# Transformer block with mixture of experts: weights as the stationary operand in gate and up, and f16 down products for the last 22 token tiles

## The reference, cut to what matters

```python
x = layernorm(x + attention(x))                  # 4 x 512 tokens, 256 wide, 16 heads
probs = softmax(x @ router_w.T); top_w, top_i = top_k(probs, 2); top_w /= top_w.sum()
for e in range(8):                               # 8 experts, 512 hidden columns
    gate = x @ ws[e, :512].T
    up   = x @ ws[e, 512:].T
    h    = silu(gate) * up
    out += combine[:, e:e+1] * (h @ w2s[e].T)    # 512 -> 256
x = layernorm(x + out)
```

## Time and profile before

| | us |
|---|---|
| median of 3 runs | 513.27 |
| lowest, highest | 512.68, 515.3 |
| the profiled execution, its own time | 515.15 |
| its span | 513.3 |
| mean granted TensorE clock | 0.947 |
| PE busy, PEld busy | 433.3, 264.0 |
| DVE, ACT, POOL busy | 334.8, 313.9, 244.5 |

### The profile page before, as it was taken

How to read it: one execution, slowest core, us unless ns; L and a number is a source line. 1 busy time by engine, 2 the same in 40 slices (tenths; PEclk the granted TensorE clock), 3 DMA queues, 4 the chain that set the end, 5 groups by cost and what they waited for, 6 DMA issues and landing times.

```text
span 513.3 us, 9836 instructions
## 1 busy us (share of the span) xinstructions
PE 433.3 (84%) x3058; PEld 264.0 (51%) x3058; DVE 334.8 (65%) x1184; ACT 313.9 (61%) x460; POOL 244.5 (48%) x332
## 2 busy tenths in 40 slices
PE   1999898999796999889973899999999999999700
PEld 0555444445453555445532567666666666666500
DVE  7156987876779887977698424577657666762234
ACT  0486549997866677665997167555535666653115
POOL 0063411123565487555825375644555665554322
PEclk9999969999999999979996799999999999999955
DMA  8368899822246214412321024333343333343254
GB/s 274 69 166 246 258 353 330 255 77 63 63 123 213 93 52 141 122 41 85 124 83 32 10 35 91 73 66 49 53 63 53 59 57 55 62 63 43 28 167 173
DMA packets 32978, 57.25 MB, mean 112 GB/s; under 512 B 5025, under 2 KB 23585, under 8 KB 31394
## 3 DMA queue, kind: packets, MB, share of 16 engines
q1 hardware_dynamic: 18306, 39.60, 24.6%
q0 software_dynamic: 7488, 10.27, 12.9%
q10 hardware_dynamic: 7136, 6.77, 4.2%
HBM read 38.64 MB, written 17.97 MB: 110 GB/s over the span
## 4 chain that ended last, share of the span: by engine, by line
PE 44%; DVE 23%; DMA 18%; issue 8%; ACT 6%; POOLq 1%; ACTq 0%; POOL 0%; SPq 0%; DVEq 0%
DMA sum_rows<-PT,IDXA 16%; PE PS L1587 9%; DVE PS L995 8%; PE PS L298 6%; PE PS L1614 5%; PE PS L1366 4%; PE PS L1405 4%; PE PS L1440 3%; PE PS L1387 2%; PE PS L305 2%; ACT PT L779 2%; DVE W L1132 2%; PE PS L1606 2%; PE PS L1459 1%; ACT W L817 1%
## 5 line engine op out<-in xcount | busy, mean ns | idle before, releaser
L995 DVE CUSTOM_DVE_ANT_0 PS<-PS,CB 128x512 f32<-128x512 f32 (+3 forms) x256 | 121.2, 516 | 35.2 <-PE PS L1366 33.9
L1587 PE MATMUL PS<-W,PT 128*128 x468 | 114.9, 382 | 4.0 <-issue 3.9
L779 ACT ACTIVATE PT<-PS 128x1024 f32<-128x1024 f32 x80 | 81.3, 1021 | 36.8 <-PE PS L1388 36.3
L730 POOL DMA_INDIRECT sum_rows<-PT,IDXA x39 | 62.1, 1593 | 57.6 <-DMA sum_rows<-PT,IDXA 21.4
L1366 PE MATMUL PS<-KQ 96*128 96x512 bf16 (+3 forms) x256 | 64.5, 316 | 13.1 <-DVE MX L995 11.9
L1587 PEld LDWEIGHTS PS<-W,PT 128*128 128x128 f16 x468 | 43.8, 98 | 43.2 <-issue 6.5
L1387 PE MATMUL PS<-KQ 104*128 104x512 bf16 (+3 forms) x256 | 60.8, 308 | 0.4 <-ACT PT L779 0.4
L714 POOL DMA_INDIRECT KQ<-x_rows,IDXA x39 | 40.0, 1027 | 30.4 <-DVE WS L1249 18.1
L1405 PE MATMUL PS<-PT,VA 128*32 128x256 f32 (+3 forms) x512 | 45.0, 446 | 4.7 <-ACT PT L779 4.7
L1388 PE MATMUL PS<-CB 128*128 128x128 bf16 x256 | 48.1, 223 | 0.0
L1366 PEld LDWEIGHTS PS<-KQ 96*128 96x128 bf16 x256 | 20.0, 100 | 46.3 <-DVE MX L995 33.4
(11 more groups left out here) (230 smaller groups left out, 891.4 us busy)
## 6 DMA issues: line engine op xcount, KB each, us to landing
W<-w1T SPq DMA_DIRECT2D x8, 1024.0 KB, 8.5
qk_parts<-W SPq DMA_DIRECT2D x32, 192.0 KB, 3.2
KQ<-qk_parts SPq DMA_DIRECT2D x32, 192.0 KB, 2.9
KQ<-qk_parts SPq DMA_DIRECT2D x64, 64.0 KB, 3.0
x_rows<-X1S ACTq DMA_DIRECT2D x4, 516.0 KB, 3.6
W<-xT SPq DMA_DIRECT2D x4, 512.0 KB, 6.7
KQ<-qk_parts SPq DMA_DIRECT2D x16, 128.0 KB, 3.0
sum_rows<-X ACTq DMA_DIRECT2D x4, 512.0 KB, 3.2
```

The source lines that it names most:

```text
L730: pool.indirect_dma_start(acc_dram, bass.IndirectOffsetOnAxis(ap=IDXA[:, j, 0:1], axis=0), YS[j % TRIO], None, compute_op=ALU.add).then_in ...
L779: act.activation(PT[n][:, :], STb[slot_of(k, n)].rearrange("p a n -> p (a n)"), ACT.Exp).then_inc(s["exp"], 1)
L995: last = dve.tensor_tensor_reduce(src, src, maskS[:, TT * P - w:], 1.0, LOW, ALU.add, ALU.max, MX[p][:, h, i:i + 1])
L1587: last = mm(dst, XGT[j % TRIO][:, x_part, k, :], w1h[:, bass.ds(at, UNIT)], start=(k == x_part == w_part == 0), stop=(k == KC - 1 and x_pa ...
```

## The change

- **Gate and up.** The operands change places: a block of 128 weight columns is stationary and the 128 token columns of `XGT` are streamed. 24 matmuls of 128 columns replace 6 of 512, twice per tile. The result has the hidden columns on the partitions, so the product DVE makes is already what down needs.
- **No transposes of the hidden part.** The 4 f32 or 8 f16 transposes of a tile and the copies out of them are gone, and so are the row maximum and its reciprocal.
- **Down.** Tiles 0 to 16 keep the f32 product. Tiles 17 to 38 (17 to 33 before) take the three f16 products; their input is scaled by a bound for each expert that `bounds` makes on DVE once, from the squares of the weights.
- **Order.** down(j-1) follows up(j) in every tile, and `add_result(j-1)` in every step of POOL. ACT's `down_squares` and `down_high` stand ahead of the last batch's other steps.

```diff
-SPLIT_FROM = 17
-LAST = NTILES - 5
-NSPLIT = LAST - SPLIT_FROM
-HSCALE = 2.0 ** -14
+SPLIT_FROM = NEARLY
+NSPLIT = NTILES - SPLIT_FROM
 N2 = FF // P * NX * E // 512
+HBOUND = 2.0 ** 8
...
-                if 1 <= j <= SPLIT_FROM or j > LAST + 1:
+                if j:
                     add_result(j - 1)
-                elif SPLIT_FROM + 2 <= j <= LAST:
-                    add_result(j - 2)
-                elif j == LAST + 1:
-                    add_result(j - 2)
-                    add_result(j - 1)
-                if j == 5 + 1:
+                if j == 6:
...
             def hidden_high(j):
-                i = j - SPLIT_FROM
-                act.wait_ge(f["ri"], i + 1)
-                act.activation(HHI[i % 2], HH, ACT.Copy, scale=RI[:, i:i + 1]).then_inc(f["hhi"], 1)
-
-            def hidden_columns(j):
-                act.wait_ge(f["th2"], j - SPLIT_FROM + 1)
-                act.wait_ge(f["yp"], j)
-                act.activation(HTH[:, 0, :, :].rearrange("p k t -> p (k t)"), HPh[0], ACT.Copy).then_inc(f["hta"], 1)
+
+                act.wait_ge(f["h"], j + 1)
+                if j >= SPLIT_FROM + 2:
+                    act.wait_ge(f["yp"], j - 1)
+                act.activation(HHI[j % 2], HH, ACT.Copy).then_inc(f["hhi"], 1)
...
+            for j in range(SPLIT_FROM, NTILES):
                 silu(j)
                 if j + 1 < NTILES:
                     columns(j + 1)
-                if j == LAST + 1:
-                    split_result(LAST - 1)
-                result(j - 1)
-            result(NTILES - 1)
+                if j == SPLIT_FROM:
+                    result(j - 1)
+                hidden_high(j)
+                if j > SPLIT_FROM:
+                    split_result(j - 1)
+            split_result(NTILES - 1)
...
+            def bounds():
+
+                dve.memset(STEP9[:, :, 0:1], 1.0)
+                dve.memset(STEP9[:, :, NX:NX + 1], 0.0)
+                link(dve.tensor_tensor(STEP9[:, :, 1:NX], CT[:, 0:NX - 1].unsqueeze(1).broadcast_to([P, NSPLIT, NX - 1]),
+                                       jidx[:, 0:NSPLIT].unsqueeze(2).broadcast_to([P, NSPLIT, NX - 1]), ALU.is_le))
+                link(dve.tensor_tensor(PICK8[:, :, :], STEP9[:, :, 0:NX], STEP9[:, :, 1:NX + 1], ALU.subtract))
+                link(dve.tensor_tensor(PICK8[:, :, :], PICK8[:, :, :], S8[:, :].unsqueeze(1).broadcast_to([P, NSPLIT, NX]), ALU.mult))
+                link(dve.tensor_reduce(SJ[:, :], PICK8[:, :, :], AX.X, ALU.add))
+                dve.wait_ge(s["sc2"], 2)
+                dve.tensor_scalar(WSJ[:, :], SJ[:, :], CC[:, :], None, ALU.mult)
+                link(dve.reciprocal(RSJ[:, :], SJ[:, :]))
+                link(dve.tensor_scalar(HSJ[:, :], RSJ[:, :], HBOUND, CW[:, :], ALU.mult, ALU.mult))
...
-                if i == 0:
-                    dve.wait_ge(f["th"], SPLIT_FROM)
-                else:
+                if i:
                     dve.wait_ge(f["hlo"], i)
-                dve.scalar_tensor_tensor(HH, U, CW[:, :], SIL, ALU.mult, ALU.mult).then_inc(f["h"], 1)
-                dve.wait_ge(f["h"], j + 1)
-                link(dve.tensor_reduce(HM[:, i:i + 1], HH, AX.X, ALU.max, apply_absolute_value=True))
-                link(dve.tensor_scalar(HB[:, i:i + 1], HM[:, i:i + 1], 1e-30, HSCALE, ALU.max, ALU.mult))
-                dve.reciprocal(RI[:, i:i + 1], HB[:, i:i + 1]).then_inc(f["ri"], 1)
-                dve.wait_ge(f["ws"], j + 1)
-                dve.scalar_tensor_tensor(WS2[:, i:i + 1], WS[:, j:j + 1], HB[:, i:i + 1], CC[:, :], ALU.mult, ALU.mult).then_inc(f["ws2"], 1)
+                dve.scalar_tensor_tensor(HH, U, HSJ[:, i:i + 1], SIL, ALU.mult, ALU.mult).then_inc(f["h"], 1)
 
             def hidden_low(j):
 
-                i = j - SPLIT_FROM
-                dve.wait_ge(f["hhi"], i + 1)
-                dve.scalar_tensor_tensor(HLO[i % 2], HH, RI[:, i:i + 1], HHI[i % 2], ALU.mult, ALU.subtract).then_inc(f["hlo"], 1)
-
-            def hidden_columns(j):
-
-                dve.wait_ge(f["th2"], j - SPLIT_FROM + 1)
-                dve.wait_ge(f["yp"], j)
-                dve.tensor_copy(HTH[:, 1, :, :].rearrange("p k t -> p (k t)"), HPh[1]).then_inc(f["htd"], 1)
+                dve.wait_ge(f["hhi"], j - SPLIT_FROM + 1)
+                if j >= SPLIT_FROM + 2:
+                    dve.wait_ge(f["yp"], j - 1)
+                dve.tensor_tensor(HLO[j % 2], HH, HHI[j % 2], ALU.subtract).then_inc(f["hlo"], 1)
...
+                dve.scalar_tensor_tensor(HT[j % 2], U, CW[:, :], SIL, ALU.mult, ALU.mult).then_inc(f["h"], 1)
                 if j == 0:
                     post(B - 1, 1, TB[1])
-                dve.wait_ge(f["th"], j + 1)
-                if j:
-                    dve.wait_ge(f["yp"], j)
-                dve.tensor_copy(HT.rearrange("p k t -> p (k t)"), HP).then_inc(f["ht"], 1)
...
             def half(j, e, dst, n, done):
 
-                for k in range(KC):
-                    for x_part, w_part in ((0, 0), (0, 1), (1, 0)):
-                        at = (e + k * NX) * (4 * UNIT) + (2 * n + w_part) * UNIT
-                        last = mm(dst, XGT[j % TRIO][:, x_part, k, :], w1h[:, bass.ds(at, UNIT)], start=(k == x_part == w_part == 0), stop=(k == KC - 1 and x_part == 1))
+                for c in range(FF // P):
+                    for k in range(KC):
+                        for w_part, x_parts in ((0, (0, 1)), (1, (0,))):
+                            at = (e + k * NX) * (4 * UNIT) + (2 * n + w_part) * UNIT + c * P
+                            for x_part in x_parts:
+                                last = mm(dst[:, c * P:(c + 1) * P], w1h[:, bass.ds(at, P)], XGT[j % TRIO][:, x_part, k, :],
+                                          start=(k == x_part == w_part == 0), stop=(k == KC - 1 and w_part == 1))
                 last.then_inc(done, 1)
...
-            def hidden_T(j):
+            def down(j, e):
                 pe.wait_ge(f["h"], j + 1)
-                if j:
-                    pe.wait_ge(f["ht"], j)
-                for k in range(FF // P):
-                    last = nc.tensor.transpose(HP[:, k * P:(k + 1) * P], HH[:, k * P:(k + 1) * P], ident)
-                last.then_inc(f["th"], 1)
-
-            def down(j, e):
-                pe.wait_ge(f["ht"], j + 1)
                 if j:
                     pe.wait_ge(f["ys"], j)
                 for k in range(FF // P):
-                    last = mm(YP[:, 0:E], HT[:, k, :], W2[k][:, bass.ds(e * E, E)], start=(k == 0), stop=(k == FF // P - 1))
+                    last = mm(YP[:, 0:E], HT[j % 2][:, k * P:(k + 1) * P], W2[k][:, bass.ds(e * E, E)], start=(k == 0), stop=(k == FF // P - 1))
                 last.then_inc(f["yp"], 1)
 
-            def split_hidden_T(j):
...
+            def split_down(j, e):
                 i = j - SPLIT_FROM
-                if i:
-                    pe.wait_ge(f["hta"], i)
-                    pe.wait_ge(f["htd"], i)
-                else:
-                    pe.wait_ge(f["ht"], SPLIT_FROM)
                 pe.wait_ge(f["hhi"], i + 1)
                 pe.wait_ge(f["hlo"], i + 1)
-                for r, part in enumerate((HHI[i % 2], HLO[i % 2])):
-                    for k in range(FF // P):
-                        last = nc.tensor.transpose(HPh[r][:, k * P:(k + 1) * P], part[:, k * P:(k + 1) * P], IDH[:, :])
-                last.then_inc(f["th2"], 1)
-
-            def split_down(j, e):
-                i = j - SPLIT_FROM
-                pe.wait_ge(f["hta"], i + 1)
-                pe.wait_ge(f["htd"], i + 1)
                 pe.wait_ge(f["ys"], j)
                 if i == 0:
                     pe.wait_ge(s["lo2"], N2)
                 for k in range(FF // P):
-                    for h_part, w_part in ((0, W2H), (0, W2L), (1, W2H)):
-                        last = mm(YP[:, 0:E], HTH[:, h_part, k, :], w_part[k][:, bass.ds(e * E, E)],
-                                  start=(k == 0 and h_part == 0 and w_part is W2H), stop=(k == FF // P - 1 and h_part == 1))
...
+                    for w_part, h_parts in ((W2H, (HHI, HLO)), (W2L, (HHI,))):
+                        for h_part in h_parts:
+                            last = mm(YP[:, 0:E], h_part[j % 2][:, k * P:(k + 1) * P], w_part[k][:, bass.ds(e * E, E)],
+                                      start=(k == 0 and w_part is W2H and h_part is HHI), stop=(k == FF // P - 1 and w_part is W2L))
...
+            for j in range(NTILES):
+                if j == NEARLY:
+                    pe.wait_ge(s["tab"], 2)
                 e = expert(j)
                 gate(j, e)
-                rows_T(j + 1)
+                if j + 1 < NTILES:
+                    rows_T(j + 1)
                 if j == 0:
                     out_proj(r, 0, (s["atc"], r * 2 + 1), TB[0])
                 up(j, e)
                 if j == 0:
                     out_proj(r, 1, (s["atc"], r * 2 + 2), TB[1])
-                if j:
+                if 1 <= j <= SPLIT_FROM:
                     down(j - 1, e_before)
```

(63 more changed lines are left out.)

74 lines of the change are left out of this document (12 added, 62 removed).

## The result

| | before | after |
|---|---|---|
| median of 4 runs, us | 513.14 | 551.26 |
| lowest, highest | 512.68, 515.3 | 550.31, 552.48 |
| ratio of the times, 95% interval | | 1.0735 (1.0697 to 1.0774) |
| profiled execution, its own time | 515.15 | 552.48 |
| its span | 513.3 | 550.7 |

Ratios leave out single runs more than 1.5% over the fastest of their own kernel (one of the four of e2_fused, three of the twelve of e8_fused_again); medians and ranges are of all runs. The kernel before was measured again beside the experiments and had 515.29 us beside e1 to e4 and 514.24 beside e5 to e8, so a difference between an experiment and the kernel after is sure to some 2 us only.

The account below looks back on a forecast made before the run. PE's sequencer was to bound the expert part: 289.7 + 91.8 (17 plain tiles) + 123.9 (21 split) + 1.5 + 2.5 = 509.4, last scatter-add at 510.2, 20.9 us later than before. Forecast 534 us, range 524 to 550.

Parts of the forecast that it names:

- What bounds: Expert part: PE's sequencer decides, with 32 register instructions a tile for gate and up in place of 8, 124 ns each.
- Start of tile 1: Value load of tile 1, no longer held by tile 0's hidden part: 289.7 us, bounds 288.5 and 291.8.
- The working of a tile: Sum of the sequencer's work in one tile: 5.90 us for a split tile, 5.40 for a plain one.
- Three distances make 0.36 to 0.38 us, 124 ns each: Price of a register instruction in gate and up, read from one trace window; 32 by 0.124 is 3.97 us a tile.
- Extras: PE's work beside the tiles (out projection, routing, counts, a few stalls): 2.5 us, bounds 0 and 6.
- The scatter chain is off the path: Scatter-adds into `sum_rows` no longer set the pace, since tiles of 5.4 and 5.9 us are over 4.59.
- its scatter-add starts 0.8 later: After the last down ends at 509.4, the last scatter-add starts 0.8 us later, at 510.2.
- The 81 ns a pair of the Trainium skill: Rule for sustained 128-column pairs, against the 56 ns used: plain tiles array-bound at 5.84 us, forecast 541.
- The array is the bound: Rival: 124 ns is waiting for a queue slot; plain tiles 4.64 us, split ones 4.59, about 501 us; 6%.
- pairs go slower: Rival: over long runs pairs exceed 56 ns, weight loads no longer hidden; 562 us at 98 ns, 538 at 77; 10%.
- The clock: Rival: the granted clock falls to 1.2 GHz as the array is busy; 8 us a tile, over 600 us; 2%.
- PE's instructions arrive too slowly: Rival: a split tile has some 175 instructions on PE against 96, and their arrival limits it; 550 us; 3%.

Follow-up runs that it names:

- e2_fused: Kernel after with gate and up addresses computed four at a time, 17 register instructions a tile in place of 32: 508.05 us, ratio to before 0.9859.
- e8_fused_again: The kernel of e2_fused measured once more in five rounds, 12 runs: 507.18 us, ratio to before 0.9838.
- e1_static: Kernel after with gate and up reading expert 0's weights at constant addresses in every tile, same matmuls: 507.72 us, ratio to before 0.9857.
- e4_more_pairs: Kernel after with sixteen more weight load and matmul pairs a tile at addresses already in registers, results unused: 555.52 us, ratio to before 1.0785.
- e5_plain: Kernel after with the plain f32 down product in all tiles but the last: 541.54 us, ratio to before 1.0535.
- e3_before_cut: Kernel before with its 512 streamed weight columns cut into four blocks of 128, each with its own address: 567.39 us, ratio to before 1.1015.
- e7_fused_noscatter: The kernel of e2_fused without the scatter-adds, a POOL memset in their place: 493.04 us, ratio to before 0.9591.
- e6_noscatter: Kernel after without the 39 scatter-adds, a one-column POOL memset in their place: 544.38 us, ratio to before 1.059.

## Why the prediction was right and where it failed

**What bounds.** Right. Register instructions stand 124 ns apart in the kernel after: the median of 1171 neighbours, with its quarters at 124 and 125, with one matmul or two behind them, and in e4_more_pairs, with two behind each, too. Taking 15 of 32 away (e2_fused) gives back 43 us, taking all away (e1_static) as much, and adding 24 to the kernel before (e3_before_cut) takes 52. That e1_static and e2_fused come out at the same time is in part chance: in both the scatter chain of the prediction, its 4.59 us a tile, stands behind the saving, but e2_fused without it (e7_fused_noscatter) keeps 4.60 us a tile, so there the sequencer needs as much as the chain.

**Start of tile 1.** 289.7 forecast, 289.9 measured. That it agrees to 0.2 is luck: in the experiments with the changed order this load starts between 287.7 (e5_plain) and 291.1 (e7_fused_noscatter).

**The working of a tile.** Right as a floor. If for each of the sequencer's steps in a tile the shortest distance to the next over 19 split tiles is taken, and these are added up, it is 5.90 us, the sum of the prediction; the same for the plain tiles of e5_plain is 5.42, against 5.40.

**The step that failed: "Three distances make 0.36 to 0.38 us, 124 ns each", carried over to all 32.** It was read in one place without a gap. Some distances are longer by 15 to 155 ns, most by 30 to 90. In the split tiles between 396 and 515 us there are 98 of them in 19 tiles, and the mean tile is 6.25 where the floor is 5.90: 0.35 us a tile. The trace of before had them too, under the array's work, where they cost nothing; I measured the distances in a gapless stretch and did not ask for the mean over many. By 37 tiles it is 12.7 us of the 16.7.

**Extras.** 2.5 forecast. The 17 periods of the plain part have 99.8 us: 17 by 5.42 is 92.1, gaps of 0.33 make 5.6, and 2.1 is left. Right.

**The second step that failed: "The scatter chain is off the path", "its scatter-add starts 0.8 later".** That holds up to tile 37. From the last value load to the last scatter-add the prediction has 5.90 + 1.5 + 0.8 = 8.2 us; it is 12.1. Kernel after, timeline of all engines at the end:

```profile
520.22 0.75 DVE L1268 SCALAR_TENSOR_TENSOR PT<-PS,HSJ,PT 128x512 f32<-128x512 f32 x1 [3.72 <-PE PS L1558]
...
521.00 0.63 ACT L916 ACTIVATE PT<-PT 128x512 f16<-128x512 f32 x1 [2.27 <-DVE PT L1268]
...
521.66 0.69 DVE L1275 TENSOR_TENSOR PT<-PT 128x512 f16<-128x512 f32 x1 [0.70 <-ACT PT L916]
...
522.56 0.39 PE L1591 MATMUL PS<-VR,PT 128*128 x2 [0.95 <-DVE PT L1275]
...
524.08 0.47 ACT L922 ACTIVATE PT<-PS,WS 128x256 f32<-128x256 f32 x1 [1.96 <-PE PS L1591]
```

In every other tile the chain product, high part, low part (the 2.5 us that I costed at nothing) is hidden by a whole gate and up; behind the last up there is only down(37), and PE stands 0.95 us for the low part. Then down(38) follows down(37) by 2.4 us and not by 6.2, so its result, ready at about 524.6, finds the scatter-add of tile 37 on its way from 522.39, and goes out at 526.94, some 2 us late. Without the chain, in e6_noscatter, the same way takes 9.8 us and not 12.1, so 2.3 of the 3.9 are the chain's. The prediction named the cover of the first chain and the pace that keeps the second off the path, and asked for neither at the last tile. All of it, the gaps in that stretch included, is 3.9 us.

So 0.2 + 0.3 (the plain floor) + 12.7 - 0.4 + 3.9 is the missing 16.7. The pace is set by what the prediction named; the gaps were put at 0 and are 12.7 us, and at the last tile two overlaps that it took for granted, of the hidden part's chain and of the scatter-adds, were missing, for 3.9.

**The 81 ns a pair of the Trainium skill** ("TensorE: Matmul & The Clock Gate", "Back-to-back issue gap") would have put the forecast at 541, nearer to the result, for a reason that the runs exclude: e1_static holds 56 ns over 24 pairs.

**The rivals.** "The array is the bound" and "pairs go slower" are excluded by e1_static and e4_more_pairs. The clock is at 1.00 from 300 to 515 us, so it did not fall; that is the higher of its two levels, 2.4 GHz. "PE's instructions arrive too slowly" is the one that names a time near the result (550). As a limit on the pace it is excluded by e4_more_pairs too, which brings 32 more instructions a tile (16 weight loads, 16 matmuls) through in 6.30 us against 6.26. As a cause of the gaps it stays possible, though they do not follow the count of instructions.

**What the gaps are stays open.** Three in four come 1.0 to 1.2 us behind the one before in the kernel after, and within gate and up mostly exactly eight of the sequencer's steps behind it. In e4_more_pairs and e3_before_cut it is eight steps as well. Eight register instructions with their pairs are 32 instructions in the kernel after and 40 in e4_more_pairs, so the "every 32 instructions" of that run's expectation is out. Counted over a tile by the same shortest distances they are 0.35 us in the kernel after, 0.39 in e4_more_pairs, 0.35 in e6_noscatter, 0.35 in e3_before_cut and 0.14 in e7_fused_noscatter, where most are about 1.5 us and ten or eleven steps apart. So it is not the scatter-adds, and not the number of matmuls (16 more pairs between the same addresses leave the spacing at 1.0 to 1.2). e7_fused_noscatter has both fewer register instructions (25 in place of 40 a tile) and a shorter tile (4.6 us in place of 6.25), so no run decides whether the gaps go with the one or the other.

**What the profile was to show.** Threes of pairs at 83 ns, register instructions at 124 ns, scatter-adds waiting for ACT: as foretold (79 to 93 ns). Value loads 5.4 and 5.9 apart: 5.87 and 6.26. "PE named issue on the chain": no; the profile calls it PE, since the records of the matmuls overlap the holes between them.

## What to carry to other kernels

A matmul whose address comes from a register costs PE's sequencer one instruction for each new address, and this adds up beside the array: before cutting matmuls finer, count the addresses of a tile, multiply by the distance of two such instructions, and compare with the array's time. Computing several addresses together halves their number at once. When a pace is read off a trace, take the mean over a long stretch beside the shortest distance, and go through the last tile by itself, since what covers a chain everywhere else is missing there.

## What the runs showed of the hardware that I had not expected

- A register instruction of six operations lasts 74 ns and takes 132 or 153 ns of the sequencer (e2_fused), one of the small ones 46 ns and 124: the operations are cheap, the instruction is dear.
- A pair of weight load and matmul behind an address already computed costs the sequencer about 7 ns or less (624 of them, 4.3 us; by the traces, 0.04 us for 16).
- The sequencer has small gaps that add 6% (0.35 of 5.90 us) when it works through register instructions without a pause, and 3% (0.14 of 4.42) in the version with fewer.
- The distance of two dependent scatter-adds, where the landing is what is waited for, is mostly 4.45 to 4.7 us: 4.59 at the end of the kernel before, 4.55 in the kernel after, 4.52 in e2_fused.
